# The diagonal of the recurrence's matrix A, made from sums per head instead of masked products

## The reference, cut to what matters

```python
def step(S, inp):
    rt, kt, vt, wt = inp
    kv = kt[..., :, None] * vt[..., None, :]
    y = jnp.einsum('bhi,bhij->bhj', rt, S + u[None, :, :, None] * kv)
    S = wt[..., None] * S + kv
    return (S, y)
```

## Time and profile before

| | us |
|---|---|
| median of 3 runs | 3330.21 (3326.12 to 3333.70) |
| profiled execution, its own time | 3334.78 |
| its span | 3333.0 |
| PE busy | 2892.8 (87%) |
| DVE busy | 2403.5 (72%) |
| POOL busy | 1454.7 (44%) |
| ACT busy | 1314.1 (39%) |

### The profile page before, as it was taken

One profiled execution on the slowest core, in us unless ns is written; L12 is line 12 of the kernel. 1 busy time (PEld: TensorE's weight loads), 2 busy tenths in 40 slices (PEclk: granted clock), 3 DMA queues, 4 the chain that ended last, 5 costly groups with the idle time before them and its releaser, 6 DMA issues.

```text
span 3333.0 us, 46581 instructions
## 1 busy us (share of the span) xinstructions
PE 2892.8 (87%) x16832; PEld 1782.4 (53%) x16832; DVE 2403.5 (72%) x4593; ACT 1314.1 (39%) x2753; POOL 1454.7 (44%) x1644
## 2 busy tenths in 40 slices
PE   2398989989899898999889898898988989899898
PEld 1135565355653666445663457635566355653567
DVE  4485687767877678766778658786587866877666
ACT  0164314733247323463225532365313743247322
POOL 0134463345624456234552436434463344623454
PEclk9699999999999999999999999999999999999999
DMA  4700024000240003300051002400024000240000
GB/s 133 131 2 2 19 39 97 2 1 20 41 95 2 1 20 65 71 2 10 14 88 45 2 10 40 101 7 2 19 39 97 2 1 19 40 84 2 1 1 14
DMA packets 70611, 114.97 MB, mean 34 GB/s; under 512 B 9451, under 2 KB 62731, under 8 KB 64187
## 3 DMA queue, kind: packets, MB, share of 16 engines
q1 hardware_dynamic: 67091, 110.72, 16.8%
q10 hardware_dynamic: 3264, 0.79, 0.1%
HBM read 74.69 MB, written 33.65 MB: 33 GB/s over the span
## 4 chain that ended last, share of the span: by engine, by line
PE 50%; DVE 24%; POOL 13%; issue 5%; ACT 3%; DMA 3%; SPq 0%; DVEq 0%; POOLq 0%; ACTq 0%
PE PB L1396 6%; PE PB L1410 6%; PE PB L1483 6%; PE PB L1426 6%; PE PB L1498 5%; DVE mxp L1085 4%; DVE arena L1265 4%; PE PB L1540 3%; DVE arena L1274 2%; PE PB L1575 2%; DVE attn L1007 2%; POOL rstd L601 2%; PE PB L1565 2%; DMA arena<-augT 2%; PE PB L1370 2%
## 5 line engine op out<-in xcount | busy, mean ns | idle before, releaser
L1085 DVE TENSOR_REDUCE mxp<-PB 128x1 f32<-128x512 f32 (+3 forms) x1216 | 723.2, 651 | 150.8 <-PE PB L1399 96.3
L838 ACT ACTIVATE arena<-PB 128x512 f32<-128x512 f32 (+3 forms) x1536 | 658.2, 512 | 390.5 <-PE PB L1410 342.3
L1396 PE MATMUL PB<-arena 96*128 96x512 bf16 (+3 forms) x1536 | 463.0, 343 | 49.7 <-DMA arena<-parts 31.6
L1410 PE MATMUL PB<-arena 99*128 99x512 bf16 (+3 forms) x1536 | 444.9, 335 | 51.7 <-DMA arena<-augT 27.0
L694 POOL TENSOR_TENSOR hl<-arena,hh 128x512 fp32r<-128x512 f32 x192 | 251.6, 1311 | 316.9 <-ACT hh L865 313.9
L1483 PE MATMUL PB<-xh,wgu 128*128 128x512 f32 x768 | 318.9, 415 | 31.5 <-DVE xl L1141 18.8
L1426 PE MATMUL PB<-arena 128*32 128x512 f32 (+3 forms) x3072 | 326.5, 499 | 8.5 <-POOL arena L670 8.5
L1483 PE MATMUL PB<-xl,wgu 128*128 128x512 f32 x768 | 312.0, 406 | 0.0
L1396 PEld LDWEIGHTS PB<-arena 96*128 96x128 bf16 x1536 | 151.2, 100 | 282.8 <-DVE mxp L1085 95.7
L714 POOL TENSOR_TENSOR arena<-arena,xT 128x512 f32<-128x512 f32 x160 | 184.1, 1174 | 261.8 <-DVE arena L1207 261.8
L670 POOL TENSOR_SCALAR_AFFINE_SELECT arena<-arena 128x512 f32<-128x512 f32 x256 | 162.0, 635 | 295.3 <-ACT arena L838 267.7
(11 more groups left out here) (143 smaller groups left out, 5437.9 us busy)
## 6 DMA issues: line engine op xcount, KB each, us to landing
arena<-parts SPq DMA_DIRECT2D x112, 256.0 KB, 9.3
parts<-arena SPq DMA_DIRECT2D x192, 128.0 KB
arena<-parts SPq DMA_DIRECT2D x16, 768.0 KB, 17.3
arena<-in_x SPq DMA_DIRECT2D x16, 512.0 KB, 7.2
arena<-parts SPq DMA_DIRECT2D x16, 512.0 KB, 19.5
xres<-in_x SPq DMA_DIRECT2D x16, 512.0 KB, 4.5
out<-xres SPq DMA_DIRECT2D x16, 512.0 KB, 13.7
wgu<-arena SPq DMA_DIRECT2D x2, 768.0 KB, 4.5
```

What stands on the lines that cost most here:

```text
L838: act.activation(pt[:, U % 3, h, 0:n], bank(b, "score", t)[:, 0:n], ACT.Exp, scale=DH ** -0.5).then_inc(act_emptied, 1)
L1085: dve.reduce_max(mxp[:, k // 2 % 2, hs[0]:hs[-1] + 1, col:col + 1], bank(b, "max", t)[:, 0:n * len(hs)].rearrange("p (h n) -> p h n", n=n) ...
L1396: last = mm(ps, qst[0:AUG, i // 4, HG * (k // 2) + h, 128 * (i % 4):128 * (i % 4) + 128], kst[0:AUG, s0 // HALF, HG * (k // 2) + h, 0:n], ...
L1410: mm(ps[:, 0:n], kst[0:AUG + 3, j // 4, h, 128 * (j % 4):128 * (j % 4) + 128], qst[0:AUG + 3, f, h, HALF - n:HALF], start=True, stop=True) ...
```

## The change

VectorE multiplies r and k elementwise into a new tile `rk` (in the place of `ku`): `weigh(0)` for the first half of the tokens, after `mixed(7)`, and `weigh(1)` for the second, where `ku` was made. For this ScalarE copies r once more, whole, into `rk`, in `r_out`. TensorE does 16 products with 128 columns of `rk` as weights and the two columns of `usel` moving; `usel` holds u of one head in each column, zero in the other head's partitions, and is written once by GpSimd. So one bank gets all the sums: 128 tokens of a chunk on partitions, 32 columns for 16 chunk halves and 2 heads. ScalarE copies the bank to `dsum` and writes 32 blocks of A, each as identity times one column of `dsum`. This sets the zeros too, so the memset of A goes. VectorE's masked copies of the first level wait block by block for ScalarE (`diag_set`), no longer for its own copies of the diagonal. The plan has one `diag` use in place of eight, and it is emptied by ScalarE.

```diff
-        add(b, "diag", range(8), "dve")
+        add(b, "diag", (0,), "act")
-        ku = ct(region(11264, 2048))
+        rk = ct(region(11264, 2048))
+        dsum, usel = region(HIGH + 13312, 32), region(HIGH + 13344, 4).rearrange("p (c h) -> p c h", c=NC)
...
@@ GpSimd
                     wait_filled(pool, b, "dn1", 3)
+                    if b == 0:
+                        pool.memset(usel, 0.0).then_inc(usel_set, 1)
+                        pool.wait_ge(usel_set, 1)
+                        for h in (0, 1):
+                            p = slice(64 * h, 64 * h + 64)
+                            pool.tensor_scalar(usel[p, :, h:h + 1], vec[p, 7:8, :].rearrange("p k c -> p c k"),
+                                               1.0, 1.0, ALU.mult, ALU.mult).then_inc(usel_set, 1)
...
                     wait_filled(pool, b, "vb", 3)
-                    pool.memset(A, 0.0).then_inc(a_zeroed, 1)
@@ ScalarE, r_out
                             act.activation(qd[64:128, c, 1, HALF * f:HALF * f + HALF], bank(b, "r", n)[64:128, :],
+                                           ACT.Copy)
+                            act.activation(rk[:, c, HALF * f:HALF * f + HALF], bank(b, "r", n)[:, :],
                                            ACT.Copy).then_inc(act_emptied, 1)
@@ ScalarE, after v_out(1)
+                    wait_filled(act, b, "diag", 0)
+                    act.activation(dsum, bank(b, "diag", 0)[:, 0:32], ACT.Copy).then_inc(act_emptied, 1)
+                    wait_emptied(act, b, "diag", 0)
+                    for k in range(2 * NT):
+                        for h in (0, 1):
+                            last = act.activation(A[:, k // NT, k % NT, h, :], ident[:, :], ACT.Copy,
+                                                  scale=dsum[:, 2 * k + h:2 * k + h + 1])
+                        last.then_inc(diag_set, 1)
@@ VectorE
+                    def weigh(f):
+                        for n in (2 * f, 2 * f + 1):
+                            a = rk[:, n % 2, HALF * f:HALF * f + HALF]
+                            wait_emptied(dve, b, "k", n)
+                            dve.tensor_tensor(a, a, kk[:, n % 2, HALF * f:HALF * f + HALF], ALU.mult).then_inc(rk_done, 1)
...
                     mixed(7)
+                    weigh(0)
                     mixed(8)
...
-                    for c in range(NC):
-                        wait_emptied(dve, b, "k", 2 + c)
-                        dve.tensor_scalar(ku[:, c, :], kk[:, c, :], vec[:, 7, c:c + 1], None, ALU.mult).then_inc(ku_done, 1)
-                    dve.wait_ge(a_zeroed, b + 1)
-                    for n in range(8):
-                        c, q = n // 4, n % 4
-                        wait_filled(dve, b, "diag", n)
-                        a = A[:, c, 2 * q:2 * q + 2, :, :].rearrange("p n h t -> p (n h) t")
-                        dve.copy_predicated(a, dmask[:, :].rearrange("p (a t) -> p a t", a=1).broadcast_to([128, 4, 128]),
-                                            bank(b, "diag", n)[:, :].rearrange("p (a t) -> p a t", a=4)).then_inc(dve_emptied, 1)
+                    weigh(1)
                     dve.wait_ge(tot_done, LEVELS * (b + 1))
...
                                 else:
-                                    wait_emptied(dve, b, "diag", 7)
+                                    dve.wait_ge(diag_set, 2 * NT * b + 4 * (2 * c + q) + 4)
@@ TensorE
                     wait_emptied(pe, b, "r", 3)
-                    for n in range(8):
-                        c, q = n // 4, n % 4
-                        pe.wait_ge(ku_done, 2 * b + c + 1)
-                        wait_bank(pe, b, "diag", n)
-                        for a in (0, 1):
-                            ch = 2 * q + a
-                            last = mm(bank(b, "diag", n)[:, 256 * a:256 * a + 256].rearrange("p (h t) -> p h t", h=2),
-                                      ku[:, c, 128 * ch:128 * ch + 128], qd[:, c, :, 128 * ch:128 * ch + 128],
-                                      start=True, stop=True)
-                        last.then_inc(filled, 1)
+                    pe.wait_ge(usel_set, 3)
+                    wait_bank(pe, b, "diag", 0)
+                    for f in (0, 1):
+                        for c in range(NC):
+                            pe.wait_ge(rk_done, 4 * b + 2 * f + c + 1)
+                            for ch in range(4 * f, 4 * f + 4):
+                                last = mm(bank(b, "diag", 0)[:, 2 * (NT * c + ch):2 * (NT * c + ch) + 2],
+                                          rk[:, c, 128 * ch:128 * ch + 128], usel[:, c, :], start=True, stop=True)
+                    last.then_inc(filled, 1)
```

More of the change, by code:

```diff
@@ L339, in build @@
         S = region(HIGH + 12288, 1024).rearrange("p (c n j) -> p c n j", c=NC, n=NT)
-        assert HIGH + 13312 <= LAST
+        assert HIGH + 13348 <= LAST
         zT = xT[:, :, 1:1 + T]
@@ L396, in build @@
         qd_zeroed = sem("qd_zeroed")
-        a_zeroed = sem("a_zeroed")
-        ku_done = sem("ku_done")
+        diag_set = sem("diag_set")
+        rk_done = sem("rk_done")
+        usel_set = sem("usel_set")
         tot_done = sem("tot_done")
```

## The result

Four runs of the changed kernel gave a median of 3297.7 us (3296.2 to 3298.7), beside 3328.2 for the kernel before. The ratio is 0.991, with a 95% interval of 0.989 to 0.992: 25 to 37 us faster. The forecast was 3290, with a range of 3281 to 3312. Beside the experiments the changed kernel was timed twice more, with ratios of 0.988 (0.986 to 0.990) and 0.989 (0.987 to 0.990). The kernel before took 3336.3 and 3335.7 us there, so the gain was 40 and 38 us, against 30 here.

A forecast was written before the change was run, and what follows sets the result against it. TensorE was busy 87% and held half of the chain, DVE and POOL 37%. 7 x 5.2 + 3.9 - 0.5 gave 40 us, all reaching the end: 3290 us from the median of 3330.2, range 3281 to 3312.

The forecast's parts named there:

- The path: Before the levels: memset (3.5 us), masked copies (5.0) and wide products go; levels start 5.2 us earlier in seven batches.
- Narrow products: On TensorE between v and the levels: sixteen at 0.22 us each, ends 0.1 and 0.26, giving 6.0 and 4.8 us.
- `weigh(1)`: On DVE, before the second eight narrow products: two products of 1.0 us each, 2.0 against the 1.90 of `ku`.
- `weigh(0)` and the copies of r: On DVE 1.4 to 2.1 us, on ScalarE 0.6 us per copy; to be covered by idle time.
- The delay of 0.3 us for `low`: On VectorE: copies of r in `r_out(1)` push `mid`, so `low`, then `weigh(1)`, start about 0.3 us later.
- ScalarE: I took 0.27 us a block: ScalarE's 32 blocks of A: one every 0.27 us, in time up to 0.30, so VectorE does not wait.
- rival 2: TensorE's clock falls at the narrow products: 1.9 to 2.8 us a batch, 3305 to 3312 us; chance 0.16.
- 7 x 5.2 + 3.9: Levels' earlier start: 5.2 us in each of seven batches, 3.9 in the last, which has no next batch's work.
- rival 1: ScalarE's blocks don't overlap, 0.38 to 0.41 us each: 2.5 to 3.4 us back per batch, 3310 to 3317; chance 0.13.
- rival 3: An engine behind the levels is late for its own reason and the gain is lost: 3325 to 3335; 0.06 with rival 5.
- rival 4: ScalarE's blocks make VectorE wait beyond the 5.2 us won, from 0.47 us a block; 3360 at 0.59; chance 0.05.
- rival 5: Levels don't shift because `rk` is late, `weigh(1)` ending 5 us later, at 412; 0.06 together with rival 3.

The follow-up runs named there:

- The zeros alone: The kernel before with A zeroed by ScalarE, not by GpSimd's memset; wide products and masked copies stay: 3330.8 us against 3334.1, ratio 0.999.
- the run with 96 columns: The changed kernel with usel padded with zeros, so each narrow product streams 96 columns instead of 2: 3293.5 us, ratio 0.987 to the kernel before.
- the split: The changed kernel with the first half's eight narrow products moved in front of v's last products: 3293.0 us, ratio 0.986 to the kernel before.
- The run held up: The changed kernel with ScalarE delayed after dsum by three waited-for copies of 2048 columns, 5.8 us: 3339.3 us, ratio 1.002 to the kernel before.

## Why the prediction was right

**The path.** It said that memset, masked copies and wide products go, that TensorE's narrow products are late next, and that the whole shift reaches the end. The first two hold in the trace; the third holds for the sum, by a piece of luck told below. The zeros alone gave 3 us, so the memset was not the price; TensorE's products in front of the levels decide their start in every kernel here but the one that leaves the narrow ones out, where `weigh(1)` does.

**The terms.** Narrow products: 0.22 us each, measured 3.63/16 = 0.227. A slip stands at the slow end: with 0.26 the sixteen would end at 408.4 and not 408.3, which leaves 4.7 us and not 4.8; it changes nothing here. `weigh(1)`: 2.0 us beside GpSimd, measured 1.90. `weigh(0)` and the copies of r cost nothing that shows: the `mixed` behind `weigh(0)` waits for TensorE as before, 0.68 us instead of 3.11. The delay of 0.3 us for `low` didn't come: `weigh(1)` starts 3.62 us after v's start (403.50 - 399.88), where `ku` started 3.63 after it. ScalarE: I took 0.27 us a block and it was 0.296. The mis-sized part is the pointer: 0.05 us from L906, 0.09 measured. Two smaller errors stand beside it: the 0.03 for an SBUF source didn't come (0.294 with an immediate, against 0.300 from PSUM), which took part of the miss back, and the overlap was 0.09 (0.387 - 0.296) and not 0.11, which added to it. The Trainium skill's page "ScalarE: Activation LUTs", section "What ACT_TABLE_LOAD costs", gives about 93 ns for a pointer operand; immediate and pointer differ by (75.7 - 52.1)/256 = 0.092 us here, so the page agrees and my term did not. It didn't matter, since the last block was ready in time, but this was close: with a full clock it was ready 0.2 to 0.3 us before VectorE's copy (0.22 to 0.24 in the run with 96 columns, 0.3 in the split), where 0.27 us a block had promised 0.9. The run held up shows what lies beyond.

**The term that was off** is the clock. The forecast's 40 us had the clock at its full level, with rival 2 at 0.16: the levels' first products at the lower level, 1.9 to 2.8 us a batch, 3305 to 3312. It came, and its mechanism is shown by two runs; its price at the place was 12.3/8 = 1.5 us in each batch, below the 1.9 to 2.8 reckoned. Between v's last product and the first update of q the forecast had 40.3 us less over the eight batches (7 x 5.2 + 3.9). With the clock full, in the run with 96 columns, it was 42.9 (89.9 - 47.0), and in the changed kernel 31.7. The result, 3298, lies between forecast and rival. I gave rival 2 too small a chance: sixteen products with 2 columns are the kind of work by which the earlier trace rows shows the clock to fall, short transposes between waits, and I weighed it as the less likely.

That the whole came nearer to the forecast than the place did is luck. In the profiles the changed kernel is 39 us shorter, with 31.7 at the place; 4.3 more lie behind y, where the first fall of the clock came 22 to 23 us after y in six of seven batches before and 8 us after it in six of seven now, the same two places as in the run with 96 columns. The prediction had no such term. The medians differ by 30 us in the first call and by 40 and 38 in the other two, so how near the 40 were depends also on the call.

**Rivals 1, 3, 4 and 5.** ScalarE's blocks overlap (one every 0.296 us, each 0.387 long), so rival 1 falls; so does rival 5, as `weigh(1)` ended at 405.40 and not at 412. No engine behind the levels gave the gain back as a whole, but a few microseconds of it move with the clock's other falls. Rival 4's threshold is borne out: a block every 0.47 us would mean the last one 5.4 us later than at 0.296, and 5.8 us of delay gave a ratio of 1.002.

## What to carry to other kernels

A long wait in the profile is worth only what the next-latest condition leaves; ask for each wait that goes what ends second. Narrow products on TensorE took the same time with 2 and with 96 columns, and a stretch of narrow ones, or of idleness, also costs the clock of the work behind it: put it between wide products. A gain at one place can move the clock's falls behind it and lose part of itself there, so compare stage by stage before trusting a local gain. A block of short instructions on an idle engine is free only until its last one is needed, and even a few of them moved to another idle engine can decide.

## What the runs showed of the hardware that was not expected

Products with 2 moving columns and with 96 take the same time (3.63 and 3.71 us for sixteen), yet only the latter keep the granted clock at 1.00 there; padding with zeros cost 0.08 us. With 15 of 16 products gone and TensorE idle 2.05 us the clock still fell in five of eight batches. A fall that comes 22 to 23 us behind y instead of 8 goes with a stretch to the next scores that is about 1 us longer (71.4 to 71.8 us, 70.3 to 70.7). A pointer scale costs ScalarE 0.092 us in each instruction back to back. And VectorE's two updates of q of the second level took 3.34 us after a wait of 0.47 us and 2.42 without it: what lengthens them I can't say, since GpSimd's work stands at other points beside them too; the loss that went with a small wait was three times its length.
